# Decoder kernel: all four score units of a token tile read by VectorE in the even slot, probabilities ring of 12 units instead of 8

## The reference

```python
x = x + _L0_attn_ref(_layernorm(x), ...)     # stage gqa: signed weights, 32 heads of 16, 8 key heads
x = x + _L0_xattn_ref(_layernorm(x), ctx, ...)  # heads of 128
x = x + _L0_ffn_ref(_layernorm(x), ...)      # sparse feed-forward
x = x + _L1_attn_ref(_layernorm(x), ...)     # stage two, first half: 32 heads of 16, one key head, alibi
x = x + _L1_xattn_ref(_layernorm(x), ctx, ...)  # stage two, second half: 32 heads of 16, 8 key heads, mask
x = x + _L1_ffn_ref(_layernorm(x), ...)      # experts
```

```python
scores = jnp.einsum('bhqd,bhkd->bhqk', q, k) / np.sqrt(HEAD_DIM)   # two: plus alibi, or masked
attn = jax.nn.softmax(scores, axis=-1)
out = jnp.einsum('bhqk,bhkd->bhqd', attn, v)
```

## Time and profile before

| | us |
|---|---|
| median of 3 runs | 2214.14 (2213.44 to 2216.16) |
| the profiled execution | 2213.81 |
| its span, first to last instruction | 2212.0 |
| `gqa` with scores, about | 28 to 203 |
| 128-wide-head attention and feed-forward | 203 to 1704 |
| `two` with scores, about | 1704 to 2122 |
| experts, rest | 2122 to 2212 |

### The profile page before, as it was taken

The page is one execution under the profiler, slowest core; times in us unless marked ns, Lnnn a source line. Parts: engine busy times, 40 slices in busy tenths (PEclk is TensorE's granted clock), DMA queues, the critical chain, the costliest instruction groups (busy, mean ns, idle before and its releaser), DMA issues. The chain is left out here.

```text
span 2212.0 us, 45005 instructions
## 1 busy us (share of the span) xinstructions
PE 2118.3 (96%) x18686; PEld 1718.5 (78%) x18686; DVE 1344.8 (61%) x2350; ACT 1028.0 (46%) x1754; POOL 902.6 (41%) x675
## 2 busy tenths in 40 slices
PE   6997999999999999999999999999998899999998
PEld 5665888888887888888888877888887677777766
DVE  6985544443334453444433558797785788888856
ACT  5774553545535455354543552111102667667632
POOL 2787241432414414143241345122122668778611
PEclk9998999999999999999999999999999899999999
DMA  4000111110112101111010123000002100100002
GB/s 168 2 21 21 48 33 55 39 47 32 40 39 77 58 21 39 39 39 58 21 40 36 44 66 98 1 0 0 0 1 76 31 7 21 50 27 11 2 1 77
DMA packets 23374, 82.06 MB, mean 37 GB/s; under 512 B 4112, under 2 KB 6288, under 8 KB 17040
## 3 DMA queue, kind: packets, MB, share of 16 engines
q1 hardware_dynamic: 23184, 79.33, 10.6%
HBM read 74.08 MB, written 4.19 MB: 35 GB/s over the span
## 5 line engine op out<-in xcount | busy, mean ns | idle before, releaser
L2644 PE MATMUL xat_TP<-shared_rounded 128*128 128x512 f32 x1024 | 321.6, 395 | 0.1
L2316 POOL TENSOR_TENSOR xat_T<-xat_T,xat_mask 128x512 f32<-128x512 f32 x64 | 82.1, 1295 | 479.3 <-DVE xat_T L2406 479.3
L104 PE MATMUL xat_G<-xat_xnT_hi,shared_rounded 128*128 128x512 f32 x768 | 244.5, 391 | 0.0
L2303 POOL TENSOR_TENSOR shared_rounded<-shared_landing,shared_rounded 128x2048 fp32r<-128x2048 f32 x39 | 179.5, 4609 | 152.4 <-ACT shared_rounded L2160 152.4
L2644 PEld LDWEIGHTS xat_TP<-shared_rounded 128*128 128x128 f32 x1024 | 188.3, 188 | 44.6 <-issue 6.2
L2644 PE MATMUL xat_TP<-shared_rounded,xat_oT_lo 128*128 128x512 f32 x512 | 199.6, 390 | 0.0
L2397 DVE RECIPROCAL xat_q_inv_rms<-xat_OT 128x16 f32<-128x16 f32 x32 | 8.3, 258 | 304.7 <-PE xat_OT L2569 304.7
L104 PE MATMUL ffn_H<-shared_rounded 128*128 128x448 f32 (+1 forms) x816 | 178.8, 368 | 3.7 <-DVE ffn_h_kept L1469 2.5
L1401 POOL TENSOR_TENSOR ffn_one_hot<-ffn_one_hot,ffn_block_rank 128x448 f32<-128x448 f32 x64 | 75.3, 1176 | 253.6 <-DVE ffn_one_hot L1450 253.6
L1377 ACT ACTIVATE shared_rounded<-ffn_TP 128x384 fp32r<-128x384 f32 x64 | 34.8, 544 | 293.4 <-PE ffn_Y L1526 246.7
L104 PEld LDWEIGHTS ffn_H<-shared_rounded 128*128 128x128 f32 x816 | 152.3, 188 | 20.8 <-DVE ffn_h_kept L1469 5.0
(11 more groups left out here) (363 smaller groups left out, 4959.5 us busy)
## 6 DMA issues: line engine op xcount, KB each, us to landing
shared_landing<-in_Cq_q SPq DMA_DIRECT2D x16, 1024.0 KB, 4.8
shared_landing<-in_Cq_o SPq DMA_DIRECT2D x16, 1024.0 KB, 4.8
shared_landing<-in_Cq_kv SPq DMA_DIRECT2D x8, 1024.0 KB, 8.2
shared_landing<-in_ctxT_paired SPq DMA_DIRECT2D x4, 1024.0 KB, 7.1
two_ctxT_raw<-in_ctxT SPq DMA_DIRECT2D x8, 512.0 KB, 4.0
shared_landing<-in_w1T SPq DMA_DIRECT2D x8, 448.0 KB, 3.7
shared_landing<-in_w SPq DMA_DIRECT2D x7, 512.0 KB, 3.7
out<-X SPq DMA_DIRECT2D x6, 512.0 KB, 3.0
```

Of the source, the lines that this page charges most:

```text
L104: last = eng.matmul(out, a, b, start=(n == 0), stop=(n == len(steps) - 1))
L2303: return eng.tensor_tensor(w[1][:, :, :], landed[:, :, :], w[0][:, :, :].bitcast(F32), ALU.subtract)
L2316: eng.tensor_tensor(T[:, n, :, :], T[:, n, :, :], mask[:, :].unsqueeze(1).to_broadcast([P, ROWS, SEQ]), ALU.add)\
L2644: last = eng.matmul(TP[m % 2][:, :], x, w, start=(n == 0), stop=(n == len(steps) - 1))
```

## The change

`RING` becomes 12. VectorE reads the scores of both slots of a token tile in the even slot: in `gqa` maxima and shifts of slot s and then of slot s+1, in `two` the four `take_scores`. Slots 0 and 1 keep their own. `find_max` of `two` stays in each slot. In odd slots no score is read. Nothing else is edited; count and shape of all instructions stay.

```diff
-    RING = 8
+    RING = 12
...
                 if s < LASTP:
-                    if sign:
-                        max_pair(s)
-                    else:
-                        take_scores(2 * s)
-                        take_scores(2 * s + 1)
-                if s < LASTP:
-                    if sign:
-                        shift_pair(s)
-                    else:
+                    for p in (s,) if s < 2 else (s, s + 1) if s % 2 == 0 else ():
+                        if sign:
+                            max_pair(p)
+                            shift_pair(p)
+                        else:
+                            take_scores(2 * p)
+                            take_scores(2 * p + 1)
+                    if not sign:
                         find_max(2 * s)
                         find_max(2 * s + 1)
```

## The result

The changed kernel takes 2222.96 us (median of 7 runs, 2221.90 to 2227.10), the kernel before, measured beside it, 2213.71 us (7 runs, 2210.67 to 2216.17). The ratio is 1.0046 with a 95% interval of 1.0034 to 1.0057, so the change costs 9 to 10 us, 0.46%. Forecast were 2222.0 us. The profiled execution of after took 2222.96 us (span 2221.2).

The account below looks back on a forecast made before the run. TensorE was taken as busiest, VectorE second, its order mattering more than its load. `gqa` 4.1 plus `two` 3.8 us, with 0.3 us for three ordinary chains, gave +8.2 us on 2213.81: 2222.0 us, range 2216 to 2230.

Parts of the forecast that it names:

- signs of being wrong: y1's wait stays under 0.5 us, a half-clock stretch appears or goes, or ordinary pairs of slots get longer.
- Slots 2 and 3 of `gqa`, +2.4 us: Slot 3's maxima and shifts go ahead of `invert` and low parts, so `k` comes 2.4 us later, nothing given back.
- Slots 8 to 10 and 16 to 18, +0.6 us each: In `gqa`, y1 comes 2.4 us later for low parts; `k`'s 1.44 us and the scores' 0.3 us waits go.
- The second path: `gqa` slots 8 to 10: late `invert` delays GpSimd's normalisation, 1.7 us at the turn, covered by y1's 2.4 us.
- Ordinary pairs: Chain from VectorE's start to the next even slot's turn, about 7.5 us, fits under an existing wait: 0 to 0.1 us each.
- single turns: `gqa`, where VectorE starts late and the chain lacks cover: 0.1 to 0.5 us at two or three places, +0.5 us.
- `two`, slot 3, +1.2 us: Same delay as in `gqa` slot 3, at 1.2 us; `k` already waits 0.60 us for low parts.
- `two`, slots 8 and 9 of 7 groups, +0.2 us each: x0's low part delays y1 by 1.2 us, x3's 1.0 us wait for the addition goes; +1.4 us over 7 groups.
- `two`, slots 62 and 63, +1.2 us: VectorE is full with the experts' first products; y2 waits for low parts behind two more reads: +1.2 us.
- The clock falls more often: Rival, chance 0.20: new waits ahead of y1 in slots 9 and 17 cost 1.4 us more each; 2224.8, up to 2230.
- All absorbed: Rival, chance 0.18: x3, `k` and scores give back all y1 loses; 2.7 us stays, 2216.5 us.
- faster: Rival, chance 0.09: low parts do not hold y1, so waits go and nothing is lost there; -5.7 us, 2208.

Follow-up runs that it names:

- low parts alone on time: Changed kernel with only the early low parts of x0 and x1 between the two pairs of reads, `invert` behind both; 2222.63 against 2211.76 us, ratio 1.0051.
- `invert` on time too: Changed kernel with `invert` and the early low parts between the two pairs of reads; 2216.83 us against 2213.66 us for the kernel before, ratio 1.0019.
- end in the old order: Changed kernel with `gqa` from slot 22 on in the order of before; 2222.89 us against 2213.66 us for the kernel before, ratio 1.0035.
- `gqa` alone: Changed kernel with early reads in `gqa` only, `two` in the order of before; 2222.94 us against 2213.82 us, ratio 1.0040.
- GpSimd relieved: Changed kernel with seven of twelve GpSimd instructions at L784 moved behind `gqa`'s last normalisation; 2234.5 us against 2211.76 us, ratio 1.0102.
- slots 2 and 3 in the old order: Changed kernel with slots 2 and 3 of both stages read in their own slots; 2222.58 us against 2213.82 us, ratio 1.0036.
- slots 8 and 16 alone: Kernel before with ring of 12 and early reads only in slots 8 and 16 of `gqa`; 2217.36 us against 2211.76 us, ratio 1.0023.
- reads last in the even slot: Changed kernel with, from slot 4 on, the second pair of reads behind `invert` and the even slot's items; 2211.71 us against 2213.66 us, ratio 0.9992.

## Why the prediction was right, and where it was not

The time came out within 1 us, and the sign and most places are as forecast, but that the sum is so close is in part luck. Some terms were too small by 3.7 us in all (`gqa` slots 2 to 4 by 1.0, slots 8 to 12 and 16 to 20 by 0.3, ordinary pairs of `gqa` by 1.3, `two` from slot 4 to 62 by 1.1). Others were too large by 2.4 us (`two` slot 3 by 0.9, its end by 1.5), and what lies ahead of slot 2 and between the two stages gives 0.4 us back. By the prediction's own signs of being wrong two came: half-clock stretches appeared and went, and two ordinary pairs of `gqa` got longer. Point by point:

* **What bounds the kernel.** Right: the wait that the edit goes at was 2.0 us in all, and the question was what stands behind the early reads. Three of the four waits for the shift in `gqa` went. Three parts of the change done alone or undone show a loss each in the traces (slots 2 and 3, slots 8 and 16, the end of `gqa`), and the ring shows none. The medians show it for the first two done alone.
* **Slots 2 and 3 of `gqa`, +2.4 us.** The step was right, `k` at 48.67 us (less the start) for 48.6; the term was too small by 1.0 us, since TensorE ran at 1.2 GHz from 45 to 55 us. Whether the wait ahead of x3, grown to 4.24 us, makes that is not shown: two kernels with the old 1.84 us have the same slow `k` and lose 0.6 and 0.7 us. The prediction had the slow `k` of before in its rows (3.45 us) and used it for the rival, not for this term.
* **Slots 8 to 10 and 16 to 18, +0.6 us each.** Right in size (0.74, 0.79) and in each part: y1's wait, `k`'s wait gone. The second path, put at 1.7 us, makes the scores of slot 10 1.8 us later where it is alone and is covered by the first where both are there, as said; but it leaves as much behind as the first. The kernel with the low parts alone on time shows it, and the one with `invert` on time too shows both gone.
* **Ordinary pairs, "0 to 0.1 each, nothing".** This step failed. The chain was 7.46 us in the first pair of the last group, about as added up; the cover was not. The prediction took the pair of the earlier trace rows as the cover of all. It is the longest of four in that group (7.04, 7.17, 7.28, 7.46 us). The others were there in the same timeline. Nor is the cover a fixed number: with the end in the old order (the kernel of that name) the first three of these pairs have 7.04, 7.43 and 7.60 us. In the second pair the chain was longer as well, 8.48 us, since GpSimd had other work (L784) ahead of its normalisation, which the sum left out. In the groups before, where products of the next group fill the slots, the chain is covered: 0.0 us from slot 4 to 8, 12 to 16 and 20 to 24. In the last group it costs 2.1 us here, 2.2 to 3.0 us in four other kernels, and where the order there is the old one the kernels show +0.1 us or less, down to -1.3 us with a slow piece of before missing. The 0.5 us for single turns and 0.3 us for three chains stood for this, in the wrong places.
* **`two`, slot 3, +1.2 us.** 0.3 us in after, 0.3 to 0.6 us in three other kernels and 1.1 us in two. `k` waits 1.54 us (0.60 us before), so the order cost its share; but of before's `k`, 5.26 us long, more had run at half clock than of after's, 4.45 us. The clock alone moves this stretch by more than the term: two kernels with the old order here are 2.3 us shorter in it than before.
* **`two`, slots 8 and 9 of 7 groups, +0.2 us each.** The mechanism was right, the places cost about 0.1 us or less. The 2.5 us of `two` come for 2.0 us from four steps in ordinary pairs (slots 6, 26, 34, 50), which the prediction put at nothing. Undoing slots 8i and 8i+1 takes the last three away, and so does `invert` between the reads. In these three the turn's weight load waits about 0.5 us for GpSimd's normalisation, so it is again the path over the late `invert`. The step in slot 6 goes with either `invert` or the low parts between; what makes it was not followed further.
* **`two`, slots 62 and 63, +1.2 us.** The size of the delay was right and its place was not: y2 waits 0.55 us as before, and the wait for the addition ahead of the transposes grew from 1.6 to 2.8 us. Behind it the trace of before has a stretch at half clock (mean 0.83 from 2110 to 2120) that after lacks, so the sum shows -0.3 us. Of the seven other kernels with the new order here three show -0.3 us too, and four 0.4, 2.3, 3.5 and 3.6 us, with half clock from this wait on; so after's trace shows a cheap case.
* **The rivals.** *The clock falls more often* is not the main account of after's profiled execution, but it is real: with the same 1.8 to 2.6 us of wait ahead of y1 it stayed in three kernels (after, `gqa` alone, GpSimd relieved) and fell in three (slots 2 and 3 in the old order, slots 8 and 16 alone, end in the old order), each time in both groups and for 1.1 to 1.3 us more, where 1.4 was the price. The Trainium skill ("TensorE: Matmul & The Clock Gate", HAM oscillation) puts such falls down to idle gaps of TensorE, longer ones than these. Here the gap alone does not decide, 1.82 us went with a fall and 2.21 us without one. Differences of this kind may be why medians differ from sums of the traces by up to 4 us; that was not shown. *All absorbed* and *faster* fall: the times do not show less than before, and of the stretches of after only the one between the stages does by over 0.3 us.
* **The sum.** +8.2 us forecast, +9.2 us found. The edited stretches up to slot 62 of `two` add 9.9 us, and the end of `two` gives 0.3 us back, for the clock that did not fall there. What lies ahead of slot 2 (+1.5) and between the stages (-1.8) makes the other -0.4 us.

What stays open: what makes the step in slot 6 of `two`; what decides whether the clock falls behind a wait of 1.8 us; how much of the slow 10 us in slots 2 and 3 of `gqa` is the change's. No version faster than the kernel before was found: reads last in the even slot come nearest, at 0.9992 (0.9982 to 1.0001), no difference.

## What to carry to other kernels

Work that is moved forward on an engine that works in order delays everything it passes; the price is the moved time at each place where somebody waits for what was passed, less the waits behind that go. Add the new chain up, but compare it with the cover of every stage, above all of the last, where less other work fills the time, not with one row: here four pairs in the same timeline differed by 0.42 us, and the one that was read made the cover look sufficient. Read the chain in each stage too: where GpSimd had other work ahead, it was 1.0 us longer. Two paths that arrive together must both be mended before anything comes back.

## What the runs showed of the hardware

* The granted clock was not the same for the same instructions behind nearly the same wait: y1 of slot 9 after 1.82 us fell to half clock, after 1.78 us it kept full clock, 0.25 us apart in time. Its 8 matmuls take 3.4 us or 2.1 us. Once slow in slot 9, slot 17 was slow too in all three kernels.
* One kernel's runs differ with the clock: those of the kernel with the ring of 12 go from 2207.65 us (mean granted clock 0.993) to 2215.65 us (0.989), with a median of 2213.67 us.
* With a wait of 4.24 us up to 47.56 us the granted clock was 0.50 from 45 to 55 us, and the product `k` in them took 3.75 us, 2.06 us at full clock. `k` took the same 3.75 us in two kernels where the wait was 1.84 us.
